# Expert outputs of a 64-image vision tower, scaled by their gate and added to the result by accumulating indirect DMAs

## The chip, the cores and the metric

The kernel runs on one core of one Trainium2 chip. The time is in device microseconds (us), the median of three runs. The engines of the core are TensorE (PE in the rows, PEld for its weight loads), VectorE (DVE), ScalarE (ACT), GpSimd (POOL) and SyncE (SP, which here only issues DMAs). Each works through its own list of instructions in order and waits for others on semaphores.

## What is computed

A small vision tower on 64 images of 3x112x112: a tokenizer (layer norm and matmul of shifted patches, 49 tokens of width 192 per image), a window attention block, and a last block with attention over the 49 tokens of an image and a mixture of eight experts. The change is in the last part of that block:

```
x = x + (o @ proj_w.T + proj_b)                      # the residual
xn2 = layernorm(x, norm2_w, norm2_b).reshape(-1, 192)
logits = xn2 @ w_gate                                # 3136 tokens, 8 experts
top_vals, top_idx = top_k(logits, 2)
gates = softmax(top_vals)
moe[t] = sum over the two chosen experts e of
         gate[t, e] * (gelu(xn2[t] @ W1[e] + b1[e]) @ W2[e] + b2[e])     # 192 -> 768 -> 192
h = h + x + moe
```

## The kernel before

Everything is in fp32. Three classes and functions write the program; class `Heads` has the last block. It begins when the window attention has left its result in memory, and goes through four stages.

**The heads stage.** 32 items, each a pair of images (128 partitions: 2 x 64, of which 49 of each 64 are real tokens), go through a software pipeline eight slots deep, written by `run_slots(eng, NP, 8, slot)` on every engine. In one slot each engine does a part of up to seven different items; the number in `item(lag)` says how many slots behind an item is. GpSimd's slot (L472 to L515) does, in this order:

- part a (newest item): six instructions of one column each, with a drain between them (L482 to L492), for the first layer norm's scale; VectorE's `bn_aggr` (L598) releases the first;
- part b (four slots behind): the multiplication with norm2's weight (L495), and, after the scatters, the addition of its bias (L507);
- part d (seven slots behind): a copy of two columns with the numbers of the destination rows into `xsrc` (L500), a drain, and two indirect DMAs (L504), which scatter the item's 128 normalized rows to the places of their first and second expert in `xs_d`, a tensor in memory sorted by expert. A row is 192 numbers and its row number (`DX = D + 1`);
- part c (three slots behind): two instructions for the second layer norm (L511, L513), for which VectorE's L591 waits, and the addition of the residual into `hall` (L515), with the semaphore `res_set`.

The gate is exp(second logit - first logit) of each token, written by ScalarE to `egs` (L758, semaphore `d_eg`). Rows that stand for no token get the row number `FAR`, which an indirect DMA skips as out of bounds.

**The turn.** VectorE counts the rows of each expert and writes a list of tiles of 128 rows (`meta`); SP and ScalarE write rows of zeros (with row number `FAR`) behind the last row of each expert (`zero_tails`); VectorE computes the two gates of each token into `gates` (L696 to L701).

**The expert stage.** 56 tiles (`NT`) of 128 rows, in a pipeline of five slots (`run_slots(eng, NT, 5, expert)`). Per tile: SP loads the rows (L963) once GpSimd has taken the row numbers of the tile two before (`xs_used`); TensorE transposes them (L913), does 12 matmuls of the first layer (L906) and 6 of the second (L921; each is shown as two, for fp32 is done in passes); ScalarE does the gelu (L801); VectorE copies the expert's first-layer weights to one of two buffers (L714, L715) and adds the output bias from PSUM into `ys` (L722, semaphore `e_out`), after the scatter of the tile two before has landed (`e_st[u]`). GpSimd (L519 to L537) waits for `e_out` and for `e_st[u]`, that of the tile two before, does an addition of one column (L527) and a copy of the row numbers (L528), drains, and scatters the tile's 128 rows to `yy_d` by an indirect DMA (L530). Then it waits for the loaded rows of a later tile and keeps their row numbers (L536, L537).

**The closing stage.** After the last scatter has landed, SP loads `yy_d` in eight groups of four items, two DMAs each (L974). ScalarE scales the second expert's rows by their gate (L814), VectorE adds the first's, scaled, and the second's to `hall` (L732, L735), and SP stores `hall` to the output (L982).

Of the kernel before, what the change touches and what calls it, by code (L numbers as in the profile page):

```python
# [16 lines left out]
F32 = mybir.dt.float32  # L17
# [31 lines left out]
NP = B // 2  # L49
# [5 lines left out]
NT = (2 * B * T + E * (ROWS - 1)) // ROWS  # L55
R = B * T + ROWS
DX = D + 1
NROW = E * R + ROWS
FAR = 1 << 20
# [18 lines left out]
C_ROW = C_TRI + P  # L78
NCONST = C_ROW + 2 * NP
# [305 lines left out]
class Heads:  # L385


    def __init__(self, nc, ctx, sb, sem, A, const, ones, colg, x2, kbd, hall, h2_d, xs_d, yy_d, out, pe1, pt1, pp, s):
        self.nc, self.A, self.const, self.ones, self.colg, self.x2, self.kbd, self.hall = nc, A, const, ones, colg, x2, kbd, hall
        self.h2_d, self.xs_d, self.yy_d, self.out = h2_d, xs_d, yy_d, out  # L390
# [5 lines left out]
        self.gates = sb("gates", [P, NP, 2])  # L396
# [35 lines left out]
        self.yl = x2[:].rearrange("p (a i k) d -> p a i k d", a=4, i=4)  # L432
        self.xdum = sb("xdum", [P, 2])
        self.yixs = sb("yixs", [P, NT], I32)
        self.yix = sb("yix", [P, 2], I32)
# [15 lines left out]
        self.o_st, self.res_set, self.d_lgo, self.xs_used, self.o_set = sem("o_st"), sem("res_set"), sem("d_lgo"), sem("xs_used"), sem("o_set")  # L451
# [3 lines left out]
        self.ew_ld, self.e_wc, self.y2_set = sem("ew_ld"), sem("e_wc"), sem("y2_set")  # L455
        self.e_st = [sem("e_st0"), sem("e_st1")]
        self.y_ld = [sem(f"y_ld{n}") for n in range(4)]
# [13 lines left out]
    def gpsimd(self, pool):  # L471
        nc, st, g = self.nc, self.st, self.nc.gpsimd  # L472
# [3 lines left out]
        def slot(item):  # L476
            a, b, c, d = item(0), item(4), item(3), item(7)
            if a:
                i = a[0]
# [16 lines left out]
            if d:  # L496
                i, u, _ = d
                pool.wait_ge(self.d_src, i + 2)
                pool.wait_ge(self.d_dst, i + 1)
                g.tensor_copy(self.xsrc[:, u, :, D:DX], self.const[:, C_ROW:C_ROW + 2 * NP].rearrange("p (i k) -> p i k", k=2)[:, bass.ds(i, 1), :].rearrange("p o k -> p k o"))  # L500
# [20 lines left out]
        def expert(item):  # L521
            if (a := item(4)):
                i, u, h = a
                pool.drain()
                pool.wait_ge(self.e_out, i + 1)
                pool.wait_ge(self.e_st[u], 16 * h)
                g.tensor_tensor(held[0], held[1], held[1], ALU.add)  # L527
                g.tensor_copy(self.yix[:, u:u + 1], self.yixs[:, bass.ds(i, 1)])  # L528
                pool.drain()
                g.indirect_dma_start(self.yy_d[:, :], bass.IndirectOffsetOnAxis(ap=self.yix[:, u:u + 1], axis=0),  # L530
                                     self.ys[:, u], None, bounds_check=2 * NP * P - 1, oob_is_err=False).then_inc(self.e_st[u], 16)
            if (b := item(1)):
                i, u, h = b
                pool.drain()  # L534
                pool.wait_ge(self.e_w[u], 16 * h + 16)
                g.tensor_tensor(held[0], held[1], held[1], ALU.add)  # L536
                g.tensor_copy(self.yixs[:, bass.ds(i, 1)], self.xs[:, u, D:DX]).then_inc(self.xs_used, 1)  # L537
        pool.wait_ge(self.dum_set, 1)
        run_slots(pool, NT, 5, expert)

    def vector(self, dve):
# [13 lines left out]
        v.memset(self.zero[:, D:DX], float(FAR))  # L555
# [139 lines left out]
        dve.wait_ge(self.d_eg, NP)  # L695
        g1, g2 = self.gates[:, :, 0], self.gates[:, :, 1]  # L696
        v.tensor_scalar(g1, self.egs[:], 1.0, None, ALU.add)
        dve.drain()
        v.reciprocal(g1, g1)
        dve.drain()  # L700
        v.tensor_tensor(g2, g1, self.egs[:], ALU.mult)  # L701
# [7 lines left out]
        def expert(item):  # L709
# [7 lines left out]
            if (c := item(3)):  # L717
                i, u, h = c
                e = dve.value_load(self.meta[0:1, 0, bass.ds(i, 1)], min_val=0, max_val=E - 1)
                dve.wait_ge(self.e_y, i + 1)  # L720
                dve.wait_ge(self.e_st[u], 16 * h)
                v.tensor_tensor(self.ys[:, u], pp[:, u, 0:D], self.b2s[:, bass.ds(e, 1), :].rearrange("p o d -> p (o d)"), ALU.add).then_inc(self.e_out, 1)  # L722
                dve.drain().then_inc(self.y_free, 1)
        run_slots(dve, NT, 5, expert)


        dve.wait_ge(self.res_set, NP)
        for n in range(NP // 4):
            dve.wait_ge(self.y_ld[n % 4], 32 * (n // 4) + 32)
            for i in range(4):  # L730
                m = 4 * n + i
                v.scalar_tensor_tensor(hall[:, m], self.yl[:, n % 4, i, 0], self.gates[:, m, 0:1], hall[:, m], ALU.mult, ALU.add)  # L732
            dve.drain()
            dve.wait_ge(self.y2_set, n + 1)
            v.tensor_tensor(hall[:, 4 * n:4 * n + 4], hall[:, 4 * n:4 * n + 4], self.yl[:, n % 4, :, 1], ALU.add).then_inc(self.o_set, 1)  # L735

    def scalar(self, act):
# [71 lines left out]

        for n in range(NP // 4):  # L810
            act.wait_ge(self.y_ld[n % 4], 32 * (n // 4) + 32)
            for i in range(4):
                y = self.yl[:, n % 4, i, 1]
                last = f(y, y, ACT.Copy, scale=self.gates[:, 4 * n + i, 1:2])  # L814
            last.then_inc(self.y2_set, 1)
# [117 lines left out]
    def sync(self, sp):  # L933
# [16 lines left out]

        sp.wait_ge(self.meta_set, 1)
# [15 lines left out]
        sp.wait_ge(self.dum_set, 1)  # L967
        for n in range(2):
            sp.wait_ge(self.e_st[n], (NT + 1 - n) // 2 * 16)

        def load(n):
            for q in range(2):
                src = self.yy_d.rearrange("(i q t k) d -> q t i k d", q=2, t=B, k=2)[q, 0:T, 4 * n:4 * n + 4]
                sp.dma_start(self.yl[q * B:q * B + T, n % 4], src).then_inc(self.y_ld[n % 4], 16)  # L974

        for n in range(4):
            load(n)
        for n in range(NP // 4):
            sp.wait_ge(self.o_set, n + 1)
            for q in range(2):  # L980
                dst = self.out.rearrange("(i q) t d -> q t i d", q=2)[q, :, 4 * n:4 * n + 4]
                sp.dma_start(dst, hall[q * B:q * B + T, 4 * n:4 * n + 4]).then_inc(self.o_st, 16)  # L982
            if n + 4 < NP // 4:
                load(n + 4)
        sp.wait_ge(self.o_st, 256)


def build(nc, A, out, stop=99):
    ctx = ExitStack()
    with ctx:  # L990
# [9 lines left out]
        def dram(name, shape, dt=F32):  # L1000
            return nc.dram_tensor(name, shape, dt, kind="Internal").ap()
# [4 lines left out]
        yy_d = dram("yy_d", [NP * P * 2, D])  # L1006
# [76 lines left out]
        heads = Heads(nc, ctx, sb, sem, A, const, ones, colg, x2, kbd, hall, h2_d, xs_d, yy_d, out, pe1, pt1, pp, s) if stop >= 4 else None  # L1083
# [435 lines left out]
def lay_out(inputs):  # L1519
# [3 lines left out]
    g = {}  # L1523
# [107 lines left out]
    c[:, C_ROW:] = (2 * (P * np.arange(NP)[None, :, None] + p[:, None, None]) + np.arange(2)).reshape(P, -1)  # L1631
# [16 lines left out]
```

## Time and profile before

| | us |
|---|---|
| median of three runs | 1308.98 |
| lowest and highest | 1304.17, 1320.23 |
| span of the profiled execution | 1321.7 |
| heads stage, first item's a part to the last one's scatter | some 608 to 980 |
| expert stage and its tail | some 990 to 1275 |
| closing stage | 1275.3 to 1321.7 |

Only the span is listed of the profiled execution, from its first to its last instruction, with nothing around it; it lies 12.7 us over the median and 1.4 us over the slowest of the three runs. TensorE's mean granted clock in it was 0.860 of full speed. Positions are us from the start of the span. In a timeline a row gives start, duration, engine, line, operation, output and inputs, and in brackets how long the engine was idle before and what released it ("issue": nothing that the profile shows, so its own drains and instruction handling). Pieces close together are merged, with their count behind the x.

### The profile page before, as it was taken

The page shows a single profiled execution, that of the slowest core. Times are in us where ns is not written, and L with a number is a line of the kernel's source. Part 1 is how long each engine was busy: PE and PEld are TensorE (multiplying, and loading weights), DVE is VectorE, ACT ScalarE, POOL GpSimd, SP SyncE. Part 2 cuts the span into 40 slices and gives each one's busy share as a digit, 9 for nine tenths or more (in the row PEclk, how much of TensorE's full clock was granted, in tenths as well). Part 3 has the DMA queues.
Part 4 walks back from the last instruction along what each step waited for, and adds up shares of the span by engine and source line. Part 5 has one row for each costly group of instructions (what it writes and reads, how often), then busy time and mean ns, then how long its engine had stood idle before and what let it go on. Part 6 is the DMA issues. An engine that isn't in the chain of part 4 may idle for free.

```text
span 1321.7 us, 25108 instructions
## 1 busy us (share of the span) xinstructions
PE 1105.6 (84%) x7254; PEld 997.7 (75%) x7255; DVE 724.3 (55%) x1825; ACT 437.7 (33%) x1092; POOL 567.1 (43%) x1075
## 2 busy tenths in 40 slices
PE   7798999899999789663999888988829999999940
PEld 4798999899998456363777777777618999999940
DVE  6566456357344888661577777787642322333224
ACT  0321221222211233421454545454304444444422
POOL 0554445444442344211355666666532444444420
PEclk9788888888888799775887889898758999999975
DMA  9545046045100200026800000000011111111114
GB/s 344 202 177 202 23 186 277 9 192 240 54 9 12 71 0 0 24 62 157 245 11 12 16 14 14 14 18 14 15 47 33 42 41 39 36 41 40 40 62 161
DMA packets 47864, 105.54 MB, mean 80 GB/s; under 512 B 6827, under 2 KB 36117, under 8 KB 45010
## 3 DMA queue, kind: packets, MB, share of 16 engines
q1 hardware_dynamic: 37986, 92.65, 20.2%
q0 software_dynamic: 5760, 9.68, 2.0%
q10 hardware_dynamic: 4080, 2.76, 0.7%
q8 instruction: 18, 0.29, 0.1%
q14 instruction: 20, 0.16, 0.0%
HBM read 87.18 MB, written 20.04 MB: 81 GB/s over the span
## 4 chain that ended last, share of the span: by engine, by line
issue 28%; PE 22%; POOLq 20%; DVE 11%; POOL 9%; DVEq 3%; DMA 3%; SPq 2%; ACT 2%; ACTq 0%
PE pe L1480 6%; POOLq L1247 5%; POOLq L534 5%; PE pe L906 4%; PE pp L921 3%; DVE prod L320 2%; POOL xs_d L504 2%; POOLq L512 2%; DVE sc L323 2%; POOLq L501 2%; DMA x<-yy_d 2%; DVEq L321 1%; POOL hall L515 1%; POOL xn L507 1%; PE pe L1484 1%
## 5 line engine op out<-in xcount | busy, mean ns | idle before, releaser
L1480 PE MATMUL pe<-wm,xm 128*128 128x193 f32 x1008 | 205.2, 372 | 1.6 <-DVEq L1333 1.6
L1480 PEld LDWEIGHTS pe<-wm,xm 128*128 128x128 f32 x1008 | 201.4, 224 | 2.7 <-issue 2.5
L906 PE MATMUL pe<-xsT,ew 96*128 96x128 f32 x1344 | 161.8, 278 | 1.5 <-ACT xsT L790 1.5
L906 PEld LDWEIGHTS pe<-xsT,ew 96*128 96x128 f32 x1344 | 159.7, 194 | 2.2 <-ACT xsT L790 2.2
L801 ACT ACTIVATE hT<-pe,eb 128x128 f32<-128x128 f32 x336 | 99.1, 366 | 154.7 <-PE pe L906 154.6
L921 PE MATMUL pp<-w2s,hT 128*128 x672 | 118.3, 326 | 0.0
L921 PEld LDWEIGHTS pp<-w2s,hT 128*128 128x128 f32 x672 | 107.8, 190 | 0.0
L530 POOL DMA_INDIRECT yy_d<-ys,yix x56 | 81.2, 1451 | 46.4 <-issue 46.4
L722 DVE TENSOR_TENSOR ys<-pp,b2s 128x192 f32<-128x192 f32 x56 | 20.0, 357 | 127.9 <-PE pp L921 127.9
L842 PEld LDWEIGHTS pp<-xT,wqk 96*96 96x96 f32 (+1 forms) x512 | 71.5, 195 | 18.7 <-issue 17.4
L504 POOL DMA_INDIRECT xs_d<-xsrc,dst x64 | 65.5, 1024 | 40.1 <-issue 40.1
L1172 ACT ACTIVATE sqt<-xm 128x2688 f32<-128x2688 f32 x14 | 34.2, 2444 | 145.2 <-DMA xm<-in_xm 42.2
L842 PE MATMUL pp<-xT,wqk 96*96 96x128 f32 (+1 forms) x512 | 79.6, 319 | 0.9 <-ACT xT L764 0.9
L1248 POOL TENSOR_TENSOR sqs<-sqs,sqt 128x448 f32<-128x448 f32 x56 | 71.2, 1271 | 8.0
L611 DVE TENSOR_TENSOR kbd<-pp,const 96x294 f32<-96x294 f32 x128 | 50.2, 451 | 27.3 <-PE pp L845 27.2
L1484 PE MATMUL pe<-ww,wv 128*128 128x193 f32 x300 | 53.4, 327 | 3.2 <-DVEq L1349 3.2
L536 POOL TENSOR_TENSOR xdum<-xdum 128x1 f32<-128x1 f32 x56 | 10.3, 184 | 101.8 <-issue 86.1
L715 DVE COPY ew<-w1s 96x1536 f32 x56 | 53.7, 958 | 0.0
L1389 DVE TENSOR_SCALAR xh<-hh,st 128x192 f32<-128x192 f32 x25 | 16.5, 662 | 67.3 <-POOL st L1269 67.3
L1484 PEld LDWEIGHTS pe<-ww,wv 128*128 128x128 f32 x300 | 49.8, 189 | 3.5 <-DVEq L1349 3.5
L714 DVE COPY eb<-b1s 128x6 f32 x56 | 9.6, 171 | 77.7 <-issue 64.7
L320 DVE TENSOR_TENSOR prod<-qkv 128x576 f32<-128x576 f32 x33 | 48.3, 1514 | 4.1 <-issue 4.1
(239 smaller groups left out, 2275.7 us busy)
## 6 DMA issues: line engine op xcount, KB each, us to landing
xm<-in_xm SPq DMA_DIRECT2D x7, 2688.0 KB, 16.6
raw<-in_xwa SPq DMA_DIRECT2D x7, 1792.0 KB, 7.2
raw<-in_xwb SPq DMA_DIRECT2D x7, 1536.0 KB, 10.4
x<-in_x SPq DMA_DIRECT2D x4, 1536.0 KB, 12.8
xs<-xs_d SPq DMA_DIRECT2D x56, 96.5 KB
x<-yy_d SPq DMA_DIRECT2D x16, 294.0 KB
w1s<-in_W SPq DMA_DIRECT2D x1, 4608.0 KB, 25.6
w2s<-in_W SPq DMA_DIRECT2D x1, 4608.0 KB, 36.5
```

Source lines behind the costliest of these rows:

```text
L320: v.tensor_tensor(prod[:, a], qkv[:, u, a:a + 1, 0:D].to_broadcast([P, 3, D]), qkv[:, u, :, D:2 * D], ALU.mult)
L504: g.indirect_dma_start(self.xs_d[:, :], bass.IndirectOffsetOnAxis(ap=self.dst[:, u, k:k + 1], axis=0), self.xsrc[:, u, k], None, bounds_ch ...
L530: g.indirect_dma_start(self.yy_d[:, :], bass.IndirectOffsetOnAxis(ap=self.yix[:, u:u + 1], axis=0), self.ys[:, u], None, bounds_check=2 * ...
L534: pool.drain()
L801: last = f(self.hT[:, u, c], pe1[:, 2 * u + c // 3, (c % 3) * ROWS:(c % 3 + 1) * ROWS], ACT.Gelu, bias=self.b1[:, u, c:c + 1])
L842: mm(pp[0:H2, g, m * P:(m + 1) * P], self.wqk[0:rows, h, g * D + m * H2:g * D + (m + 1) * H2], self.xT2[0:rows, h], start=(h == 0), stop=( ...
L906: last = mm(pe1[:, 2 * u + n // 3, (n % 3) * ROWS:(n % 3 + 1) * ROWS], self.w1[:, u, m, n * P:(n + 1) * P], self.xsT[:, m], start=(m == 0) ...
L921: last = mm(pp[:, u, 0:D], self.hT[:, u, n], self.w2s[:, bass.ds(e, 1), n * D:(n + 1) * D].rearrange("p o d -> p (o d)"), start=(n == 0), ...
L1247: pool.drain()
L1248: last = nc.gpsimd.tensor_tensor(dst, dst, src[c], ALU.add)
L1480: mm(y[:, 0:D + 1], cell(q, c), wm[:, q, c], start=(q + c == 0), stop=(q == 3 and c == KC - 1))
L1484: mm(y[:, 256:256 + D + 1], wave(wv, wv6, q), ww[:, q], start=(q == 0), stop=(q == 5))
```

## The change

Tile rows carry their gate as a 194th number. GpSimd computes it in the heads stage, the VectorE of the expert stage multiplies each output row with it, and the indirect DMA of the expert stage adds to the output tensor in memory, which SP has filled with the residual during the heads stage. `yy_d`, `gates` and the closing stage are gone. Rows for no token now have a real destination: 128 dummy rows behind the output.

In the heads stage, on GpSimd:

```diff
-DX = D + 1
+DX = D + 2
...
                 i, u, _ = d
                 pool.wait_ge(self.d_src, i + 2)
                 pool.wait_ge(self.d_dst, i + 1)
-                g.tensor_copy(self.xsrc[:, u, :, D:DX], ...)
+                pool.wait_ge(self.d_eg, i + 1)
+                g.tensor_tensor(st[:, 16:17], self.egs[:, bass.ds(i, 1)], self.ones[:, 0:1], ALU.add)
+                g.tensor_copy(self.xsrc[:, u, :, D:D + 1], ...)
             pool.drain()
             if d:
+                g.tensor_tensor(self.xsrc[:, u, 0, D + 1:DX], st[:, 16:17], self.const[:, C_NEG:C_NEG + 1], ALU.pow)
+                pool.drain()
+                g.tensor_tensor(self.xsrc[:, u, 1, D + 1:DX], self.xsrc[:, u, 0, D + 1:DX], self.egs[:, bass.ds(i, 1)], ALU.mult)
+                pool.drain()
                 for k in range(2):
                     g.indirect_dma_start(self.xs_d[:, :], ...)
```

In the expert stage, on GpSimd:

```diff
                 pool.wait_ge(self.e_out, i + 1)
-                pool.wait_ge(self.e_st[u], 16 * h)
+                pool.wait_ge(self.e_st[1 - u], 16 * (h + u))
                 g.tensor_tensor(held[0], held[1], held[1], ALU.add)
                 g.tensor_copy(self.yix[:, u:u + 1], self.yixs[:, bass.ds(i, 1)])
                 pool.drain()
-                g.indirect_dma_start(self.yy_d[:, :], ...,
-                                     self.ys[:, u], None, bounds_check=2 * NP * P - 1, oob_is_err=False)
+                g.indirect_dma_start(self.out[:, :], ...,
+                                     self.ys[:, u], None, bounds_check=B * T + P - 1, oob_is_err=True,
+                                     compute_op=ALU.add)
...
                 g.tensor_tensor(held[0], held[1], held[1], ALU.add)
-                g.tensor_copy(self.yixs[:, bass.ds(i, 1)], self.xs[:, u, D:DX]).then_inc(self.xs_used, 1)
+                g.tensor_copy(self.yixs[:, bass.ds(i, 1)], self.xs[:, u, D:D + 1])
+                g.tensor_copy(self.gxs[:, bass.ds(i, 1)], self.xs[:, u, D + 1:DX]).then_inc(self.xs_used, 1)
         pool.wait_ge(self.dum_set, 1)
+        pool.wait_ge(self.o_st, 16 * 17)
         run_slots(pool, NT, 5, expert)
```

The scatter of a tile is now issued only after that of the tile before it has landed. On VectorE:

```diff
-                v.tensor_tensor(self.ys[:, u], pp[:, u, 0:D], ..., ALU.add).then_inc(self.e_out, 1)
+                v.tensor_tensor(self.ys[:, u], pp[:, u, 0:D], ..., ALU.add)
                 dve.drain().then_inc(self.y_free, 1)
+                dve.wait_ge(self.xs_used, i + 3)
+                v.tensor_scalar(self.ys[:, u], self.ys[:, u], self.gxs[:, bass.ds(i, 1)], None, ALU.mult).then_inc(self.e_out, 1)
```

VectorE's computation of `gates` in the turn (three instructions) is removed. On SP, ahead of its wait for `meta_set`, 17 stores are added, and the loads and stores behind the last `e_st` wait are removed:

```diff
+        sp.dma_start(self.out[B * T:], self.zero[:, 0:D]).then_inc(self.o_st, 16)
+        for n in range(NP // 4):
+            sp.wait_ge(self.res_set, 4 * n + 4)
+            for q in range(2):
+                dst = self.out[0:B * T].rearrange("(i q t) d -> q t i d", q=2, t=T)[q, :, 4 * n:4 * n + 4]
+                sp.dma_start(dst, hall[q * B:q * B + T, 4 * n:4 * n + 4]).then_inc(self.o_st, 16)
         sp.wait_ge(self.meta_set, 1)
         self.zero_tails(sp, range(0, E, 2))
...
         for n in range(2):
             sp.wait_ge(self.e_st[n], (NT + 1 - n) // 2 * 16)
-        for n in range(4):
-            load(n)
-        for n in range(NP // 4):
-            sp.wait_ge(self.o_set, n + 1)
-            ...
```

The row numbers (constant `C_ROW`) now count output rows, the zero rows carry the number of a dummy row (`C_DUM`) in place of `FAR`, and the output tensor has 3136 + 128 rows, of which the first 3136 are returned.

## Rows read from the trace of the kernel before

**Rows 1.** Busy time by stage: heads, turn to the experts, experts, tail, closing stage

```profile
core 0: us, PE busy (x) PEld busy (x) DVE busy (x) ACT busy (x) POOL busy (x), PEclk, DMA share, GB/s
...
640.00:965.00 325.00, 284.07 (x2310) 238.37 (x2309) 240.07 (x873) 160.43 (x451) 193.46 (x415) 0.88 0.09 30
...
1003.50:1265.00 261.50, 261.50 (x2049) 261.50 (x2048) 77.11 (x160) 109.40 (x378) 111.32 (x266) 1.00 0.13 38
...
1275.20:1321.70 46.50, 0.00 (x0) 0.00 (x0) 18.91 (x40) 11.93 (x32) 0.00 (x0) 0.50 0.44 156
```

**Rows 2.** The closing stage in order of time: last scatter, first load, last addition

```profile
1273.05 1.00 POOL L530 DMA_INDIRECT yy_d<-ys,yix  x1 [0.82 <-issue]
1275.26 7.80 SPq L974 DMA_DIRECT2D x<-yy_d  x8
...
1315.57 0.96 DVE L735 TENSOR_TENSOR hall<-hall,x 128x768 f32<-128x768 f32 x1
```

**Rows 3.** One slot of the heads stage, GpSimd alone, in order of time

```profile
842.20 0.19 POOL L482 TENSOR_TENSOR st<-st,const 128x1 f32<-128x1 f32 x1 [0.68 <-DVE st L598]
842.53 0.55 POOL L484 TENSOR_TENSOR st<-st,const 128x1 f32<-128x1 f32 x1
843.22 0.19 POOL L486 TENSOR_TENSOR st<-st 128x1 f32<-128x1 f32 x1
843.56 0.19 POOL L488 TENSOR_TENSOR st<-st 128x1 f32<-128x1 f32 x1
...
846.35 1.08 POOL L504 DMA_INDIRECT xs_d<-xsrc,dst  x1 [0.87 <-issue]
...
850.37 0.57 POOL L513 TENSOR_TENSOR st<-st,const 128x1 f32<-128x1 f32 x1 [0.90 <-issue]
850.92 0.58 POOL L515 TENSOR_TENSOR hall<-hall,x  x1
```

**Rows 4.** First GpSimd instruction of other heads slots, with its wait

```profile
675.59 0.19 POOL L482 TENSOR_TENSOR st<-st,const 128x1 f32<-128x1 f32 x1 [3.06 <-DVE st L598]
...
686.33 0.19 POOL L482 TENSOR_TENSOR st<-st,const 128x1 f32<-128x1 f32 x1 [1.28 <-DVE st L598]
...
924.88 0.19 POOL L482 TENSOR_TENSOR st<-st,const 128x1 f32<-128x1 f32 x1 [1.84 <-DVE st L598]
```

**Rows 5.** Two items of the expert stage in order of time

```profile
1199.98 0.36 DVE L722 TENSOR_TENSOR ys<-pp,b2s 128x192 f32<-128x192 f32 x1 [2.37 <-PE pp L921]
1200.10 0.18 POOL L536 TENSOR_TENSOR xdum<-xdum 128x1 f32<-128x1 f32 x1 [1.60 <-issue]
1200.23 0.18 POOL L537 CAST yixs<-xs 128x1 f32 x1
...
1200.74 0.20 POOL L527 TENSOR_TENSOR xdum<-xdum 128x1 f32<-128x1 f32 x1 [0.34 <-DVE ys L722]
...
1201.80 0.96 DVE L715 COPY ew<-w1s 96x1536 f32 x1
1201.89 1.75 POOL L530 DMA_INDIRECT yy_d<-ys,yix  x1 [0.83 <-issue]
...
1204.26 2.81 PEld L906 LDWEIGHTS pe<-xsT,ew 96*128 96x128 f32 x24
...
1204.83 0.36 DVE L722 TENSOR_TENSOR ys<-pp,b2s 128x192 f32<-128x192 f32 x1 [2.07 <-PE pp L921]
...
1205.86 0.20 POOL L527 TENSOR_TENSOR xdum<-xdum 128x1 f32<-128x1 f32 x1 [0.28 <-issue]
...
1207.00 1.21 POOL L530 DMA_INDIRECT yy_d<-ys,yix  x1 [0.83 <-issue]
```

**Rows 6.** Tensor yy_d, all its instructions: time to landing

```profile
DMA to landing us min/median/max: 2.1/2.6/4.3
```

**Rows 7.** Chain that ended last: a load of rows from memory

```profile
990.86 1.84 DMA xs<-xs_d
```

More of the change, by code:

```diff
@@ L78 @@
 C_ROW = C_TRI + P
-NCONST = C_ROW + 2 * NP
+C_DUM = C_ROW + 2 * NP
+C_NEG = C_DUM + 1
+NCONST = C_NEG + 1
 def run_slots(eng, n, depth, slot, unroll=2):
@@ L450, in __init__ @@
         self.e_y, self.e_out, self.y_free, self.dum_set = sem("e_y"), sem("e_out"), sem("y_free"), sem("dum_set")
-        self.o_st, self.res_set, self.d_lgo, self.xs_used, self.o_set = sem("o_st"), sem("res_set"), sem("d_lgo"), sem("xs_used"), sem("o_set")
+        self.o_st, self.res_set, self.d_lgo, self.xs_used = sem("o_st"), sem("res_set"), sem("d_lgo"), sem("xs_used")
         self.h_ld = [sem(f"h_ld{n}") for n in range(4)]
@@ L454, in __init__ @@
         self.e_w = [sem("e_w0"), sem("e_w1")]
-        self.ew_ld, self.e_wc, self.y2_set = sem("ew_ld"), sem("e_wc"), sem("y2_set")
+        self.ew_ld, self.e_wc = sem("ew_ld"), sem("e_wc")
         self.e_st = [sem("e_st0"), sem("e_st1")]
-        self.y_ld = [sem(f"y_ld{n}") for n in range(4)]
     def zero_tails(self, eng, experts):
@@ L554, in vector @@
         dve.drain()
-        v.memset(self.zero[:, D:DX], float(FAR))
+        v.tensor_copy(self.zero[:, D:D + 1], const[:, C_DUM:C_DUM + 1])
         dve.drain().then_inc(self.init, 2)
@@ L693, in vector @@
         dve.drain().then_inc(self.meta_set, 1)
[L695 to L701, printed above, removed]
         for n in range(2):
@@ L721, in expert @@
                 dve.wait_ge(self.e_st[u], 16 * h)
-                v.tensor_tensor(self.ys[:, u], pp[:, u, 0:D], self.b2s[:, bass.ds(e, 1), :].rearrange("p o d -> p (o d)"), ALU.add).then_inc(self.e_out, 1)
+                v.tensor_tensor(self.ys[:, u], pp[:, u, 0:D], self.b2s[:, bass.ds(e, 1), :].rearrange("p o d -> p (o d)"), ALU.add)
                 dve.drain().then_inc(self.y_free, 1)
+                dve.wait_ge(self.xs_used, i + 3)
+                v.tensor_scalar(self.ys[:, u], self.ys[:, u], self.gxs[:, bass.ds(i, 1)], None, ALU.mult).then_inc(self.e_out, 1)
         run_slots(dve, NT, 5, expert)
-        dve.wait_ge(self.res_set, NP)
-        for n in range(NP // 4):
[L729 to L735, printed above, removed]
     def scalar(self, act):
@@ L808, in scalar @@
         run_slots(act, NT, 5, both)
[L810 to L815, printed above, removed]
     def tensor(self, pe):
@@ L1082, in build @@
         wins = Windows(nc, ctx, sb, sem, A, const, ones, xnT, wqkv, colg, mowT, owT, hall, base_d, h2_d, pe1, pt1, pp, s) if stop >= 2 else None
-        heads = Heads(nc, ctx, sb, sem, A, const, ones, colg, x2, kbd, hall, h2_d, xs_d, yy_d, out, pe1, pt1, pp, s) if stop >= 4 else None
+        heads = Heads(nc, ctx, sb, sem, A, const, ones, colg, x2, kbd, hall, h2_d, xs_d, out, pe1, pt1, pp, s) if stop >= 4 else None
         block = ctx.enter_context(nc.Block())
```

34 lines of the change are left out of this document (11 added, 23 removed).

## Prediction

> **What bounds the kernel now.** I read the busy time by stage first. Three stretches matter [rows 1]. In the heads stage (640 to 965) TensorE is busy 284 of 325 us, at a granted clock of 0.88, and no engine is full, so a chain through several engines sets the pace. In the expert stage (1003.5 to 1265) TensorE is busy 261.5 of 261.5 us at the full clock. In the closing stage (1275.2 to 1321.7) TensorE does nothing and the DMA engines are busy 0.44 of the time: it is loads, additions and stores with nothing beside them.
>
> Next the closing stage in order of time: the last scatter is issued at 1273.05, SP issues the first load when it has landed, at 1275.26, and the last addition starts at 1315.57 [rows 2].
>
> Then one slot of the heads stage on GpSimd [rows 3]. It begins at 842.20 and ends with L513 at 850.94; the part after L513 that matters goes by VectorE: L513 releases L591, VectorE comes to `bn_aggr` (L598), and that releases the next slot's first instruction. That wait, measured on GpSimd after its own last instruction, is 0.68 us in the slot shown. In the slot shown the loop is therefore nearly all GpSimd's: whatever is put between its first instruction and L513 lengthens the slot. In others the wait is longer (1.28, 1.84 [rows 4]); there VectorE was held up by TensorE, and GpSimd has that much to spare. Of the 24 slots whose first and last start at 686.33 and 924.88 [rows 4], 13 wait 0.68 us, two 0.73 and 0.75, nine 1.26 to 2.40.
>
> Last the expert stage [rows 5]. VectorE's L722 follows itself in 4.85 us, TensorE's pace. GpSimd: 1.15 us from L527 to the scatter (1200.74 to 1201.89), the scatter 1.75, then 2.22 to the next L527 (1203.64 to 1205.86); the next scatter takes 1.21, the last ones, where VectorE copies no weights, 1.00 [rows 2]. The long one starts inside the copy of the weights (1201.80, 0.96 us). Without overlap GpSimd's round would be 1.15 + 1.00 + 2.22 = 4.37 us, with full overlap 5.12, and it swings between the two to the mean of 4.85 that TensorE dictates. It has 0.48 us to spare, if it can move out of the copy's way.
>
> **Part by part.**
>
> *The closing stage goes:* 1321.7 - 1275.3 = 46.4 us [rows 2]. What stays is SP's wait for the last landing, which was there before. -46.4.
>
> *GpSimd's gate in the heads stage.* Per item: an addition of one column before the copy, a pow with drain, a multiplication with drain. The two last have their equals in the slot: pow to next 843.22 - 842.53 = 0.69, multiplication to next 843.56 - 843.22 = 0.34 [rows 3]. An undrained one-column instruction adds 0.13 (L536 to L537, 1200.10 to 1200.23 [rows 5]). That is 1.16; I take 1.25, since operands of the new ones have their column in a register, for which no row stands (bounds 1.16 and 1.35). It stands before the scatters (846.35), so both scatters, the bias addition and L513 are late by it: in the loop. In the 15 slots with no more than 0.07 to spare it costs 1.25 each, 18.6 together. In the nine with more to spare, the spare (wait minus 0.68) is 0.58 to 1.72 us, and what is left over sums to 2.3. In the tail of the stage, where fewer parts run, I count three slots at 1.25, 3.8. Together +25. Bounds: +15 if in half of the fast slots another engine has hidden slack; +36 if the spare time of the slow slots can't be used (27 x 1.35). `d_eg` of the item was set a slot earlier: that wait costs nothing. Behind the d part only GpSimd's own b and c parts queue; ScalarE waits for the scatters before it refills `xsrc`, late by the same 1.25 as all of the slot.
>
> *SP's stores of the residual.* 17 DMAs in the heads stage, where the DMA share is 0.09 [rows 1], each behind `res_set`. SP has nothing else queued until `meta_set`, and the last pair goes when item 31 has its residual, four slots before its scatter (part c against part d), with the whole turn behind that. 0, up to 2 if they delay scatters.
>
> *The turn.* The three `gates` instructions ran beside SP's zero rows: 0.
>
> *VectorE in the expert stage.* The multiplication of 128x192 is like L722 (0.36), and a drain of some 0.1 goes before it. The copy it delays ends at 1202.76 and the matmuls that read the copy start at 1204.26 [rows 5]: 1.5 us of cover for 0.5 us. 0 in the steady part; `e_out` is 0.5 late once, at the end: +0.5. The wait for `xs_used` is for a part that GpSimd did two slots before: 0.
>
> *GpSimd in the expert stage, own work.* One more copy: 0.13. The accumulating scatter has to read its destination too. The trace has no accumulating DMA. From below the scatter's 1.00 us stays as it is. From above: a plain row has a read and a write, an accumulating one two reads and a write; if the 1.00 us goes by that count it becomes 1.50. So the round without overlap is 4.50 to 5.00 us, against 4.85. I take 1.25 (round 4.75), nearer to neither: then 0.1 is to spare, some overlap with the copy is left that can't be avoided, and I take the round as 4.95: 0.1 x 54 tiles = +5. Bounds 0 and, with 5.00 and half of the overlap (0.38), 5.38: +0.53 x 54 = +28.
>
> *The new wait.* L527 now waits until the scatter before has landed. Queued behind it are the scatter, L536 and L537; SP's next load waits for L537. Issue to landing took 2.1 to 4.3 us, median 2.6 [rows 6]. Today's L527 comes 1.75 + 2.22 = 3.97 or 1.21 + 2.22 = 3.43 us after the scatter's start, so a landing up to 3.4 us is hidden. The round by this wait is landing + 1.15 + 0.1. For the landing of an accumulate, from below 2.6; from above a load (1.84 [rows 7]) in series with a scatter: 1.84 + 2.6 = 4.44, a round of 5.69, +0.84 x 54 = +45. I take 3.5, nearer the plain scatter, since a load of rows and the rows' read can overlap: round 4.75, hidden by the above, with occasional late ones (+3). At the end three scatters in a row cost 0.5 more each: +1.5.
>
> The Trainium skill, page "DMA: Bandwidth & Descriptors", section "Rules for kernel authors", says that nothing holds the bytes between an accumulate's read and its write, so the earlier DMA's semaphore must be waited for; no run here shows it, and it is why this wait can't be left out. The same page, "Latency and other measured facts", gives an HBM access 0.2 us on average and 2 us at high load; an estimate from it is a landing of 2.8 (hidden) or 4.6 (a round of 5.85, +54 us), and with a DMA share of 0.13 the first is nearer.
>
> The scatter's 1.00, 1.21 and 1.75 us by its overlap with the copy are the row. The Trainium skill, page "SBUF — State Buffer", section "Who interferes with whom", has it that a VectorE copy in a two-port mode locks GpSimd out for the whole instruction. By that rule, which the trace agrees with, GpSimd's extra work is partly taken back by moving out of the copy; were 1.75 and 1.21 the scatter's own times, the 0.13 alone would cost 0.1 x 54 = 5 us.
>
> **Sum**, against the span: -46.4 + 25 + 0 + 0.5 + 5 + 3 + 1.5 = -11.4, say -12. The span is 12.7 us over the median, mostly by TensorE's clock, which a median run shares less; the terms are the same there. 1309 - 12 = 1297.
>
> **The rivals.**
>
> 1. *The landing decides, and the kernel is slower.* Place: GpSimd's wait before L527. It begins to cost at a landing of 3.6 us (3.6 + 1.25 = 4.85) and decides the sign at 3.9 to 4.0, where 54 x 0.3 = 17 us have eaten the rest of the gain. At the 4.44 above: -46.4 + 25 + 45 + 2 = +26, 1335; if the eight rows of each DMA engine were not pipelined, far more. For: plain landings already reach 4.3 us. Against: the median is 2.6, and the DMA engines are idle. Chance 0.22.
> 2. *GpSimd's gate in the heads stage is hidden* (TensorE or VectorE sets the pace, or the clock is granted more often): -46.4 + 8 + 8 = -30, 1279. For: nine of 24 slots have the time. Against: the constant 0.68 in the others. Chance 0.2.
> 3. *GpSimd's software needs far longer for an accumulating scatter* (2.0 us for 1.00): a round of 5.5 to 5.8, +35 to +51, with the heads +25: +14 to +30, 1331. For: the 1.00 us is software time, by which rows it goes is unknown. Against: nothing in the trace. Chance 0.1.
> 4. *The change doesn't do what it says:* SP's stores come late and hold the expert stage back (GpSimd waits for all 17). Each stored group would have to be 20 us late. Chance 0.03, 1310.
>
> **How the numbers follow.** Forecast 0.45, rivals 0.22, 0.2, 0.1, 0.03. The forecast's own range is -27 (heads +15, experts +4) to +3, 1282 to 1312. The range is 1277 to 1335: below it little but rival 2 with free experts, above it the costlier half of rivals 1 and 3. A difference under 2% (26 us) is about what a measurement of this kernel can't tell from no change. Faster by over 2% needs heads and experts together under 20 us: rival 2 and the forecast's edge, 0.22. Slower by over 2%: the heavier part of rivals 1 and 3, 0.22. Within: 0.56.
>
> **What would show it.** No row after the last scatter's landing. GpSimd's L482 rows 11.1 us apart in most slots instead of 9.9, the 0.68 us wait unchanged. In the expert stage L722 4.9 to 5.0 us apart, TensorE no longer busy all the time; the accumulating scatter 1.2 to 1.5 us, landing 3 to 3.6. Wrong if the heads slots stay at 9.9 (rival 2), if L527 waits on the landing of a scatter in most rounds (rival 1), or if the scatter's own row grows to 2 us (rival 3).

## The result, and the profile after

The changed kernel takes 1360.35 us (median of four runs, 1354.43 to 1374.44) where the kernel before takes 1312.39 (four runs): the ratio is 1.0396, 95% interval 1.0346 to 1.0447. It is slower by 4%, and lies above my range of 1277 to 1335.

The span of the profiled execution is 1358.4 us, 36.7 longer than that of before. Busy time by stage of the changed kernel (heads; experts from the first scatter on; behind the last scatter), columns as in [rows 1]:

```profile
core 0: us, PE busy (x) PEld busy (x) DVE busy (x) ACT busy (x) POOL busy (x), PEclk, DMA share, GB/s
640.00:985.00 345.00, 289.81 (x2254) 244.59 (x2252) 240.55 (x865) 157.39 (x440) 217.53 (x497) 0.84 0.11 36
1030.30:1340.00 309.70, 275.80 (x2020) 260.31 (x2019) 96.28 (x211) 108.22 (x372) 134.34 (x313) 0.99 0.23 33
1354.50:1358.40 3.90, 0.00 (x0) 0.00 (x0) 0.00 (x0) 0.00 (x0) 1.57 (x1) 0.50 0.25 25
```

The closing stage is gone: 3.9 us stand behind the start of the last scatter, where before there were 48.7 (1273.05 to 1321.7 [rows 2]). But in the expert stage TensorE is no longer busy all the time, 275.8 of 309.7 us against 261.5 of 261.5 in [rows 1], at a clock of 0.99.

The heads stage went as foreseen. One slot on GpSimd, to be held against [rows 3]:

```profile
838.14 0.19 POOL L482 TENSOR_TENSOR st<-st,const 128x1 f32<-128x1 f32 x1 [0.68 <-DVE st L607]
...
841.23 0.19 POOL L501 TENSOR_TENSOR st<-egs,ones 128x1 f32<-128x1 f32 x1
...
841.69 0.55 POOL L505 TENSOR_TENSOR xsrc<-st,const 128x1 f32<-128x1 f32 x1
842.39 0.19 POOL L507 TENSOR_TENSOR xsrc<-xsrc,egs 128x1 f32<-128x1 f32 x1 [0.15 <-issue]
843.46 1.07 POOL L510 DMA_INDIRECT xs_d<-xsrc,dst  x1 [0.88 <-issue]
...
847.37 0.57 POOL L519 TENSOR_TENSOR st<-st,const 128x1 f32<-128x1 f32 x1 [0.80 <-issue]
...
849.55 0.19 POOL L482 TENSOR_TENSOR st<-st,const 128x1 f32<-128x1 f32 x1 [1.04 <-DVE st L607]
```

The wait before L482 is 0.68 us here too, and the gate's instructions (L501, L505, L507) put the first scatter 5.32 us behind L482, where it was 4.15. The 24 slots from the L482 at 667.10 to that at 939.63 take 272.5 us, against 249.3 (675.59 to 924.88 [rows 4]); most are 11.1 us, as against 9.9. The first expert scatter starts 424.7 us after the first L482 (605.62 to 1030.33), before 399.6 (607.84 to 1007.46): +25.1, and the stages ahead of it were 2.2 shorter.

The expert stage is where the forecast broke. A round on GpSimd and VectorE, in order of time, to be held against [rows 5]:

```profile
1179.89 1.58 POOL L536 DMA_INDIRECT out<-ys,yix  x1 [0.85 <-issue]
...
1183.74 0.18 POOL L543 TENSOR_TENSOR xdum<-xdum 128x1 f32<-128x1 f32 x1 [2.27 <-issue]
...
1184.00 0.17 POOL L545 COPY gxs<-xs 128x1 f32 x1
...
1184.50 0.19 POOL L533 TENSOR_TENSOR xdum<-xdum 128x1 f32<-128x1 f32 x1 [0.33 <-issue]
...
1185.65 1.60 POOL L536 DMA_INDIRECT out<-ys,yix  x1 [0.84 <-issue]
1185.93 0.36 DVE L724 TENSOR_TENSOR ys<-pp,b2s 128x192 f32<-128x192 f32 x1 [5.05 <-PE pp L908]
1186.50 0.32 DVE L727 TENSOR_SCALAR ys<-ys,gxs 128x192 f32<-128x192 f32 x1 [0.21 <-issue]
```

The scatter's own row is 1.58 us, 1.00 to 1.75 before; behind it GpSimd is idle for 2.27 us (it was 1.6) until L543. From scatter to scatter it is 5.76 us. From the first of the 56 scatters to the last it is 324.2 us (1030.33 to 1354.52), before 265.6: +58.6, or 5.89 us a tile for 4.83. The sum over the stages: -2.2 + 25.1 + 58.6 - 44.8 = +36.7.

Who waited, in the expert stage of the changed kernel (engine and line, releaser: us, times, longest):

```profile
POOL xdum L543 <- issue: 115.6, 52, 2.3
...
DVE ys L724 <- DMA out<-ys,yix: 34.5, 10, 3.6
POOL xdum L533 <- issue: 15.8, 52, 0.3
```

In ten rounds VectorE's L724 waits for a landing as well: it may write `ys` only when the scatter two tiles back has landed. L533 stands behind the new semaphore wait for the last landing, and it waits for no landing, only its usual 0.3 us. The 115.6 us stand before L543, the first instruction behind a drain, and the view calls them "issue": it shows no releaser. How long the scatters took to land, all 56:

```profile
DMA to landing us min/median/max: 3.4/3.6/4.3
```

3.6 us, where it was 2.6 [rows 6]. The landing I had forecast (3.5), and I had forecast it to be hidden.

### The profile page after: what moved, and what is told of

Its sections match the earlier page's. It is cut to its first block, busy times and chain, and to the rows that moved or that the text cites. A ratio compares the mean times of both kernels' runs of the same rounds, so it can differ in the third digit from the quotient of the medians.

```text
span 1358.4 us, 25446 instructions
## 1 busy us (share of the span) xinstructions
PE 1125.2 (83%) x7254; PEld 1004.1 (74%) x7255; DVE 731.0 (54%) x1838; ACT 426.7 (31%) x1060; POOL 623.2 (46%) x1227
## 4 chain that ended last, share of the span: by engine, by line
issue 32%; POOLq 26%; PE 14%; DVE 11%; POOL 9%; DVEq 3%; ACT 1%; SPq 1%; DMA 1%; ACTq 0%
POOLq L541 8%; PE pe L1455 6%; POOLq L1222 5%; POOLq L518 3%; DVE prod L322 2%; POOL xs_d L510 2%; DVE sc L325 2%; DVEq L323 1%; POOLq L506 1%; PE pe L1459 1%; POOL hall L521 1%; POOLq L485 1%; DVE pv L339 1%; POOL xn L513 1%; PE pp L829 1%
## 5 line engine op out<-in xcount | busy, mean ns | idle before, releaser
L1455 PE MATMUL pe<-wm,xm 128*128 128x193 f32 x1008 | 202.0, 368 | 1.6 <-DVEq L1308 1.6
L1455 PEld LDWEIGHTS pe<-wm,xm 128*128 128x128 f32 x1008 | 198.4, 221 | 2.7 <-issue 2.5
L908 PE MATMUL pp<-w2s,hT 128*128 x672 | 124.6, 336 | 28.0 <-issue 15.1
L536 POOL DMA_INDIRECT out<-ys,yix x56 | 99.3, 1773 | 47.4 <-issue 47.4
L724 DVE TENSOR_TENSOR ys<-pp,b2s 128x192 f32<-128x192 f32 x56 | 20.0, 358 | 174.4 <-PE pp L908 130.7
L543 POOL TENSOR_TENSOR xdum<-xdum 128x1 f32<-128x1 f32 x56 | 10.3, 184 | 129.3 <-issue 117.8
L843 PE MATMUL pe<-const,pm 128*128 128x128 f32 x192 | 29.2, 291 | 39.6 <-ACT pm L739 39.6
L717 DVE COPY ew<-w1s 96x1536 f32 x56 | 56.8, 1014 | 0.0
L843 PEld LDWEIGHTS pe<-const,pm 128*128 128x128 f32 x192 | 22.2, 147 | 45.9 <-ACT pm L739 45.8
L860 PE MATMUL pe<-vbd,pT 128*64 128x34 f32 x768 | 53.0, 247 | 1.6 <-ACT pT L749 1.6
```

The source lines that it names most:

```text
L536: g.indirect_dma_start(self.out[:, :], bass.IndirectOffsetOnAxis(ap=self.yix[:, u:u + 1], axis=0), self.ys[:, u], None, bounds_check=B * T ...
L717: v.tensor_copy(self.w1[:, u].rearrange("p h f -> p (h f)"), self.w1s[:, bass.ds(e, 1), :].rearrange("p o f -> p (o f)"))
L908: last = mm(pp[:, u, 0:D], self.hT[:, u, n], self.w2s[:, bass.ds(e, 1), n * D:(n + 1) * D].rearrange("p o d -> p (o d)"), start=(n == 0), ...
L1455: mm(y[:, 0:D + 1], cell(q, c), wm[:, q, c], start=(q + c == 0), stop=(q == 3 and c == KC - 1))
```

## The experiments

The kernel before ran beside each group of these, with medians of 1308 to 1320 us; where a ratio is given, it is to those runs. Times without a ratio are one run. The heads stage of the same code differs between profiles (391.7 to 399.0 us in e4, e5 and e7, 424.7 to 427.6 in the changed kernel, e1, e6 and e8), so I read each profile by stages as well: "heads" is from the first L482 (or the line it has there) to the first expert scatter, "experts" from that to the last scatter's start, "rest" what follows. Each stage time is from one profile.

| kernel | time | heads | experts | rest |
|---|---|---|---|---|
| before | 1312.4 | 399.6 | 265.6 | 48.7 |
| changed | 1360.4 | 424.7 | 324.2 | 3.9 |
| e1 plain scatter | 1297.0 | 427.5 | 265.7 | 2.8 |
| e2 two targets, no wait | 1360.1 | 429.3 | 327.1 | 3.9 |
| e3 gate in the kernel before | 1346.5 | 428.0 | 265.4 | 48.0 |
| e4 gate elsewhere | 1317.9 | 399.0 | 313.0 | 3.9 |
| e5 e4 and index work elsewhere | 1276.6 | 393.0 | 267.8 | 3.9 |
| e6 no drain behind the scatter | 1313.1 | 425.8 | 282.9 | 3.9 |
| e7 e5 with a plain scatter | 1260.1 | 391.7 | 265.2 | 2.7 |
| e8 half the rows | 1332.2 | 427.6 | 302.0 | 3.5 |
| e9 no wait, no drain | 1304.4 | 431.8 | 264.4 | 6.5 |
| e10 kernel before, one drain less | 1311.9 | 394.1 | 265.8 | 48.0 |
| e11 e5 and e10 | 1273.2 | 398.1 | 266.8 | 4.0 |
| e12 wait, no drain | 1325.6 | 440.4 | 268.5 | 6.4 |

First theory: the accumulating scatter costs GpSimd itself more time, in its instruction and in the drain behind it. Rivals: the new wait for the landing, the added copy, the bounds flag.

**e1, the scatter without accumulation.**

```diff
-                                     ..., oob_is_err=True, compute_op=ALU.add)
+                                     ..., oob_is_err=True)
```

> The changed kernel with the accumulation taken out of the expert scatter (the rows are written over the residual, so the sum is left out); wait, gate, copies and the bounds flag stay. Theory (an accumulating scatter costs GpSimd itself some 1.2 us more: 0.59 in the instruction, 0.6 in the drain behind it): instruction back to 1.0 to 1.75 us, landing 2.6, round 4.85 to 4.95 in place of 5.78, time some 1360 - 55 * 0.85 = 1313. Rival (the round is made by the wait for the landing, the added copy or the bounds flag): round stays above 5.5 us, time over 1345.

1296.95 us, experts 265.7. With everything of the change in place but the accumulation, the expert stage takes what it took before. (That the whole time is also my forecast for the change, 1297, is chance: the forecast had 9.5 us for the expert stage, which are not there.) The copy, the flag and the wait cost nothing beside a plain scatter; 58 us hang on the accumulation. GpSimd's rows of two rounds:

```profile
1181.86 1.52 POOL L536 DMA_INDIRECT out<-ys,yix  x1 [0.85 <-issue]
...
1185.01 0.29 POOL L542 TENSOR_TENSOR xdum<-xdum 128x1 f32<-128x1 f32 x1 [1.63 <-issue]
...
1187.00 1.02 POOL L536 DMA_INDIRECT out<-ys,yix  x1 [0.85 <-issue]
...
1189.64 0.18 POOL L542 TENSOR_TENSOR xdum<-xdum 128x1 f32<-128x1 f32 x1 [1.62 <-issue]
```

Scatter to L542 is 3.15 and 2.64 us, against 3.85 in the changed kernel.

**e2, two targets, the wait of before.**

```diff
-                pool.wait_ge(self.e_st[1 - u], 16 * (h + u))
+                pool.wait_ge(self.e_st[u], 16 * h)
-                g.indirect_dma_start(self.out[:, :], ...
+                g.indirect_dma_start((self.alt if u else self.out)[:, :], ...
```

> The changed kernel with odd tiles accumulated into a second tensor, also filled with the residual (so half of the addition is left out of the output), and with the wait of before (the scatter two tiles back) in place of the wait for the last one. Theory (GpSimd's own time per accumulating scatter is the round; the wait is hidden): round 5.7 to 5.8 us, time 1355 to 1362, GpSimd free of waits on landings. Rival (the wait for the landing makes the round): round back to 4.9 to 5.1, time some 1315.

SP fills both targets with the residual, which doubles its stores in the heads stage (in e9 and e12 too). 1360.12 us, experts 327.1: taking away the semaphore wait alone gains nothing. That speaks for the theory, but, as e6 shows, only because something else waits for the same thing.

**e3, the gate alone.** The three instructions (addition, pow, multiplication, two drains) put into the kernel before, results in a spare column.

> The kernel before with the three GpSimd instructions of the gate (addition, pow with drain, multiplication with drain) added at their place in the heads stage, their results unused. Theory (the heads stage's loop goes through GpSimd, 1.19 us a slot): slots 11.1 us in place of 9.9, +20 to +23 us on the kernel before. Rival (the heads stage of the changed kernel was longer by TensorE's clock or by SP's stores): under +8 us.

Ratio to the kernel before 1.023 (interval 1.015 to 1.031), some 30 us, with heads 428.0. The loop goes through GpSimd; the price was above my 20 to 23. Over all profiles the eight kernels with the gate on GpSimd have heads of 424.7 to 440.4 us (mean 429), the six without 391.7 to 399.6 (mean 396): 33 us, or 31 without e2, e9 and e12, where SP stores the residual twice. The granted clock, over the same 24 slots of before, of the changed kernel and of e7 (gate elsewhere), a fence each, in this order:

```profile
675.60:924.90 249.30, 222.23 (x1835) 188.17 (x1835) 189.68 (x697) 128.26 (x360) 156.24 (x337) 0.90 0.04 15
```

```profile
667.10:939.60 272.50, 233.25 (x1828) 197.54 (x1827) 194.21 (x697) 129.04 (x360) 177.88 (x408) 0.86 0.06 20
```

```profile
660.80:906.50 245.70, 217.20 (x1832) 183.32 (x1830) 190.52 (x697) 130.84 (x384) 156.35 (x336) 0.92 0.07 22
```

With longer slots TensorE is busy for a smaller part of them, and it has the lower of its two clocks, 1.2 GHz, more often (0.86 of 2.4 GHz on average against 0.90 and 0.92). Over the same slots of the other kernels it is 0.80 to 0.84 with the gate on GpSimd and 0.89 to 0.94 without. That the longer slots cause the lower clock is not shown by a run of its own.

**e8, half of the rows.** The scatter takes partitions 0 to 63 only.

> The changed kernel with the accumulating scatter over 64 of the 128 rows of a tile (half of the expert outputs is left out). If GpSimd's cost goes by the row, the instruction falls from 1.59 to about 0.8 to 1.0 us and the drain behind it from 2.2 to 1.4 to 1.7, the round to 4.85 to 5.0, time some 1315. If it is a fixed cost of each accumulating DMA, both stay and the round stays at 5.7.

In between: the instruction 1.43 us for 1.58 where no copy lengthens it, landing 3.2 for 3.6, experts 302.0. Half of the rows takes off 22 of the 58.6 us, so most of the cost is per scatter, not per row. What GpSimd's queue carried (packets, MB, share of the 16 engines' span), page of before, of the changed kernel, of e8:

```profile
q0 software_dynamic: 5760, 9.68, 2.0%
```

```profile
q0 software_dynamic: 11136, 10.39, 5.0%
```

```profile
q0 software_dynamic: 7552, 7.63, 3.5%
```

Before, 120 scatters had 48 packets each; with 64 x 48 of the heads stage taken off, an accumulating one has 144, and with half the rows 80.

**e4, the gate off GpSimd.** ScalarE writes exp(d) and exp(-d) of the logit difference d as the 194th number, VectorE makes 1/(1+w) of it per tile.

```diff
-                f(self.egs[:, bass.ds(n6, 1)], self.st[:, 12:13], ACT.Exp).then_inc(self.d_eg, 1)
+                f(x[:, 0, D + 1:DX], self.st[:, 12:13], ACT.Exp)
+                f(x[:, 1, D + 1:DX], self.st[:, 12:13], ACT.Exp, scale=-1.0).then_inc(self.d_eg, 1)
...
+                v.tensor_scalar(self.gx[:, u:u + 1], self.gxs[:, bass.ds(i, 1)], 1.0, None, ALU.add)
+                dve.drain()
+                v.reciprocal(self.gx[:, u:u + 1], self.gx[:, u:u + 1])
```

> The changed kernel with the gate off GpSimd's list in the heads stage: ScalarE writes exp(d) and exp(-d) of the logit difference d into the row (one more instruction of 0.2 us), VectorE makes 1/(1+w) of it for each tile in the expert stage (two one-column instructions). Theory (GpSimd is the loop of the heads stage): slots back to 9.9 us where TensorE's clock is full, time 22 to 30 us under the changed kernel, some 1333. Rival (ScalarE or VectorE take over the loop): under 10 us gained. The expert round stays at 5.8 in both.

1317.93 us, heads 399.0, ratio to the kernel before 1.0024 (0.9973 to 1.0075): the heads stage is back, 42 us below the changed kernel. The profiles differ by 45 us: 26 in heads, 8 ahead of it, where the code is the same, and 11 in the expert stage, which I had not expected. The 56 scatters' own rows are shorter there, 1606 ns on average against 1773, which is 56 x 0.167 = 9 us (by line, e4 and the changed kernel; ahead of the bar busy time, mean ns):

```profile
L532 POOL DMA_INDIRECT out<-ys,yix x56 | 89.9, 1606 | 47.3 <-issue 47.3
```

```profile
L536 POOL DMA_INDIRECT out<-ys,yix x56 | 99.3, 1773 | 47.4 <-issue 47.4
```

In both kernels 50 of the 56 scatters overlap VectorE's copy of the weights (0.96 us); what differs is which of the two starts first. In e4 the copy starts 0.01 to 0.53 us after the scatter in 47 of them, and both take their usual time (1.58 to 1.61 and 0.95 to 0.98 us). In the changed kernel both keep their usual time in 26 (the copy starts 0.01 us before to 0.54 after the scatter); in 11 the copy starts first, and the scatter takes 1.95 to 2.30 us; in ten it starts 0.54 to 0.73 us after the scatter, which then takes 1.92 to 1.94, and the copy 1.13 to 1.30. Why the order is another one in e4 no run shows.

**e5, GpSimd's list emptied.** VectorE picks out row numbers and gates (`e_w` wait, two one-column instructions beside the weights' copy, one more beside the bias), GpSimd keeps:

```diff
                 pool.wait_ge(self.e_out, i + 1)
                 pool.wait_ge(self.e_st[1 - u], 16 * (h + u))
                 g.tensor_tensor(held[0], held[1], held[1], ALU.add)
                 pool.drain()
                 g.indirect_dma_start(self.out[:, :], ..., compute_op=ALU.add).then_inc(self.e_st[u], 16)
```

> The kernel of e4 with the row numbers and gates of a tile picked out by VectorE, so that GpSimd's list in the expert stage is one dummy addition that holds the waits, a drain and the accumulating scatter. Theory (GpSimd's own list is the round: 0.75 for the three copies, 1.15 to the scatter, 1.59, 2.2): the list falls to about 4.6, but the wait for the landing (3.65 after the scatter's start) and 1.0 to the next one give 4.75 to 5.0; time 1276 to 1290, below the kernel before. Rival (something else holds the round at 5.8): no change against e4.

1276.58 us, ratio to the kernel before 0.9695 (0.9610 to 0.9781), nothing left out: faster than both. Now the waits name the DMA:

```profile
POOL xdum L528 <- DMA out<-ys,yix: 108.8, 54, 2.2
...
DVE ys L715 <- PE pp L902: 43.6, 54, 2.9
```

GpSimd waits 108.8 us for landings here too, but it has nothing else to do: landing (3.6) and its 1.15 us fit into TensorE's 4.85, and VectorE waits for TensorE, as before.

**e6, the drain behind the scatter removed** (the one at the head of the part with L543 to L545; the drain ahead of the next scatter's waits stays).

> The changed kernel without GpSimd's drain right behind the scatter; the drain before the next scatter's waits stays. If the 2.2 us behind the instruction are GpSimd's own work on the descriptors, they only move to the next instruction or the next drain and the round stays at 5.7 to 5.8. If they are the drain's (waiting for something that the three copies needn't), the copies move up beside it and the round falls by 0.3 to 0.7, time 1320 to 1345.

1313.05 us, experts 282.9: 41 us for one drain, far more than expected. The rows:

```profile
1178.61 1.59 POOL L537 DMA_INDIRECT out<-ys,yix  x1 [0.84 <-issue]
...
1180.00 0.43 POOL L545 TENSOR_TENSOR xdumb<-xdum 128x1 f32<-128x1 f32 x1
...
1180.26 0.40 POOL L547 COPY gxs<-xs 128x1 f32 x1
...
1182.39 0.19 POOL L534 TENSOR_TENSOR xdum<-xdum 128x1 f32<-128x1 f32 x1 [1.73 <-DMA out<-ys,yix]
...
1183.54 1.94 POOL L537 DMA_INDIRECT out<-ys,yix  x1 [0.84 <-issue]
```

The three one-column instructions (L545 to L547) start 1.39 us after the scatter does, and they run: GpSimd is not busy with the scatter. Then L534 waits, named, for the landing, 3.78 us after the scatter. So the theory falls: the time behind the instruction isn't GpSimd's work. I then took the landing of single scatters and set it beside the next instruction behind the drain. One of the changed kernel (the scatter at 1179.89, L543 at +3.85) and one of e1 (the scatter at 1187.00, L542 at +2.64):

```profile
DMA to landing us min/median/max: 3.6/3.6/3.6
```

```profile
DMA to landing us min/median/max: 2.4/2.4/2.4
```

In 17 scatters of the changed kernel, 13 of e1, 11 of e8 and 21 of the kernel before, landings from 2.4 to 4.3 us, the next instruction came 0.2 to 0.3 us after the landing, in every one. The traces say the same of all the others: in the changed kernel, the kernel before, e2, e3, e4, e8 and e10 it is 0.18 to 0.27 us in all 55 scatters of the expert stage that another instruction follows, with landings from 2.1 to 5.5 us; in e1 in 54 of 55 (0.91 in one of the last, where the next instruction is L533, which waits for VectorE too). The drain's own row does not show the wait. In the chain that ended last, behind the scatter of 1179.89 in the changed kernel, it ends with the scatter's row, and 2.12 us follow for which the view names no work:

```profile
1179.66 1.81 POOLq L541
1181.47 2.12 issue
1183.59 0.04 POOLq L542
```

L541 is the drain, L542 the semaphore wait behind it. The new theory: a GpSimd drain behind an indirect DMA waits until that DMA has landed.

**e7, e5 with a plain scatter.**

> The kernel of e5 with a plain scatter in place of the accumulating one (the addition is left out). It shows what is left when neither the heads stage nor the scatter costs anything: TensorE's round of 4.85, 46 us less closing stage, time some 1265. If the heads stage has not come back, some 1290.

1260.08 us, heads 391.7, experts 265.2: the floor. e5 loses 2.6 us to it in the expert stage.

**e9 and e12, no drain in the expert loop.** GpSimd orders the copy before the scatter by a semaphore of its own; e9 has two targets and the old wait, e12 one target and the new wait.

```diff
-                pool.drain()
...
-                g.tensor_copy(self.yix[:, u:u + 1], ...)
-                pool.drain()
+                g.tensor_copy(self.yix[:, u:u + 1], ...).then_inc(self.c_s, 1)
+                pool.wait_ge(self.c_s, i + 1)
+                g.tensor_tensor(self.xdumc[:, 0:1], held[1], held[1], ALU.add)
```

> The changed kernel with no drain on GpSimd in the expert loop (a semaphore that GpSimd gives and takes itself orders the row numbers' copy before the scatter), two targets as in e2 (half of the addition is left out of the output) and the wait for the scatter two tiles back. In every kernel so far the drain behind a scatter ended 0.22 to 0.30 us after that scatter's landing. Theory (the landing is waited for twice, by the drain and by the new semaphore wait, and only both together hold GpSimd back; without both GpSimd has some 1.6 + 1.5 us of work a round): TensorE's round of 4.85, time 1295 to 1302, as e1. Rival (the accumulate costs GpSimd the time itself): round over 5.3, time over 1325.

> As e9, but with one target and the changed kernel's wait for the last scatter's landing: nothing is left out. Theory: landing 3.6 + 0.25 to the next held instruction + 0.6 to 1.0 to the next scatter = 4.5 to 5.0 us a round; time 1298 to 1312. Rival as in e9.

e9: 1304.43 us, experts 264.4, TensorE busy throughout, with accumulating scatters of 1.6 to 2.2 us:

```profile
1032.00:1290.00 258.00, 258.00 (x2021) 258.00 (x2020) 92.52 (x210) 108.29 (x374) 161.93 (x372) 1.00 0.28 40
```

The accumulation costs nothing once nobody on GpSimd waits for its landing. e12: experts 268.5 (4.88 us a tile), so with the semaphore wait alone the landing nearly fits into TensorE's round. Its time of 1325.6 was outside what I expected, by its heads stage (440.4). There its code is that of e9 (431.8) and e2 (429.3); all three store the residual twice, although e12 uses only one target, and all three are above the 424.7 to 427.6 of the kernels that store it once. So part of it may be those stores; the rest is the spread of that stage between profiles. No run separates the two.

**e10, one drain of the heads stage in the kernel before**, the one between L511 and L513, replaced by a semaphore in the same way.

> The kernel before with one drain replaced, the one between the two one-column instructions of part c in the heads stage, by a semaphore that GpSimd gives and takes itself. It is the first drain behind the two scatters. Theory (it waits for the second scatter's landing, 2.64 us after its start): L513 0.5 to 0.7 us earlier, slots 9.3 in place of 9.9 where GpSimd is the loop, 8 to 18 us faster. Rival (GpSimd itself is busy with descriptors, or the drain costs what a semaphore costs): within 4 us of the kernel before.

The rows of e10, and below them the second scatter of the slot in [rows 3]:

```profile
846.68 0.97 POOL L505 DMA_INDIRECT xs_d<-xsrc,dst  x1 [0.30 <-issue]
...
848.22 0.20 POOL L512 TENSOR_TENSOR st<-st,const 128x1 f32<-128x1 f32 x1
848.50 0.57 POOL L514 TENSOR_TENSOR st<-st,const 128x1 f32<-128x1 f32 x1
...
850.60 0.19 POOL L483 TENSOR_TENSOR st<-st,const 128x1 f32<-128x1 f32 x1 [0.97 <-DVE st L599]
```

```profile
847.73 0.97 POOL L504 DMA_INDIRECT xs_d<-xsrc,dst  x1 [0.30 <-issue]
```

L514 (L513 of before) starts 1.82 us after the second scatter, 0.6 us before that scatter landed (2.4 us after its issue), where L513 started 2.64 us after it before (847.73 to 850.37 [rows 3]). So this drain waited for the landing too. The time: ratio 0.9971 (0.9926 to 1.0017), no difference that was measured: with 0.8 us gone from GpSimd's part, the next wait for VectorE is 0.97 us and the slot 9.7.

**e11, e5 with e10's edit.**

> The kernel of e5 with the drain of e10 replaced. Theory: 8 to 18 us under e5, so 1260 to 1268, some 4 per cent under the kernel before. Rival as in e10: as e5, 1276.

1273.22 us, ratio to the kernel before 0.9692 (0.9623 to 0.9761): as e5, within what can be told.

## Why the prediction was wrong, point by point

*The closing stage:* forecast -46.4, measured -44.8. Right.

*GpSimd's gate:* forecast +25 (bounds 15 and 36), in the pair of profiles +25.1, over all kernels +33. The mechanism was right (11.1 us slots, 0.68 us waits unchanged, e3, e4). The pair's agreement is partly luck: I let the slots with spare time absorb the 1.25 us, and did not count with a lower clock. Of the eight kernels with the gate on GpSimd the changed one has the shortest heads stage and the highest granted clock over those 24 slots (0.86, the others 0.80 to 0.84).

*SP's stores, the turn, VectorE's multiplication, the added copy:* forecast 0 or less than 1; e1 has all of them and an expert stage of 265.7 against 265.6, and e3, which has no stores, has a heads stage of 428.0 against 424.7 to 427.6. Right. e1's time of 1297 equals the forecast by chance: with its 9.5 us for the expert stage taken out, the forecast would be some 1288.

*The accumulating scatter on GpSimd:* forecast 1.25 us, bounds 1.00 and 1.50; measured 1.58, outside. But e9 shows that this alone costs nothing.

*The landing:* this is the step that failed. I wrote that today's L527 comes 3.97 or 3.43 us after the scatter's start, "so a landing up to 3.4 us is hidden". The landing was 3.6, close to my 3.5. But L527 came that late because of the landing: the drain before L536 had waited for it, and 1.6 us after each scatter were put down in my sum as GpSimd's fixed round of 4.37. With the landing in series, the round is 3.6 + 0.25 to L543, 0.76 to L533, 1.15 to the scatter: 5.76, as measured. My landing of 3.5 put in that place would have given 5.66, and 54 x (5.66 - 4.85) = +44 us where the sum had 5 + 3 for the whole of GpSimd's part. The view had called this wait "issue", and I took "nothing that the profile shows" for the engine's own time.

*Rival 1* had the price (a slower kernel by the landing in series, 5.69 us a round for 4.44) and the wrong place: it was to happen at the semaphore wait before L527. e2 takes that wait away and gains nothing, e6 takes the drain away and gains 41 us, e9 takes both and has the whole excess back. With the drains gone and the semaphore wait left (e12) the landing costs 2.9 us (268.5 for 265.6), so of that wait by itself I was nearly right. *Rival 3* (GpSimd's software) had the instruction's own row at 2.0 us; it is 1.58, and e9 carries it at no cost. *Rival 2* fell with e3. *Rival 4* did not come: SP issued the last of its stores at 981 us, and the first GpSimd instruction behind the wait for them (L543 at 1013.15) was released by the load of the first tile's rows.

The estimate that I had worked out from a figure of the Trainium skill (page "DMA: Bandwidth & Descriptors", section "Latency and other measured facts", 0.2 us for an HBM access on average) was a landing of 2.8 us; the runs show 3.6, and the measurement decides. The Trainium skill's rule on the shared port (page "SBUF — State Buffer", section "Who interferes with whom") has it that whichever of the two issues first gets the port pair for its whole instruction and blocks the other. For a scatter that starts inside VectorE's copy the trace agrees: 1.95 to 2.30 us in place of 1.58. For a copy that starts with the scatter or up to 0.5 us after it, the trace does not agree: neither takes longer (26 times in the changed kernel, 47 in e4).

## What to carry to other kernels

Idle time that a profile calls "issue" is not thereby the engine's own: before it goes into a sum as a constant, set it beside the landing of the DMA issued just before, over several instances; if the two move together, it is a wait, and it grows with the DMA. In a loop like this one, with an indirect DMA on GpSimd, keep drains out of the stretch between the DMA and its landing (a semaphore that the engine gives to itself orders two of its instructions without that wait), and give index work to another engine. And a stage whose pace is a loop through one engine's small instructions pays for each instruction added, once per slot.

## What the runs showed of the hardware that I had not expected

- Behind a GpSimd drain that follows an indirect DMA, the next instruction started 0.2 to 0.3 us after that DMA's landing, plain (2.1 to 4.5 us) or accumulating (3.0 to 5.5 us), whatever the landing was. Without the drain the next GpSimd instruction starts 1.39 us after a 1.59 us scatter does. That it is the drain that waits is concluded from this and from e6, e9 and e10; its own row in the profile ends with the scatter's.
- Clear of VectorE's copy, an accumulating scatter of 128 rows of 768 bytes lands 3.5 us after its start and a plain one to the same tensor 2.4 (e1; to `yy_d` in the kernel before 2.15). It takes 1.58 instead of 1.02 us to issue, and makes 144 packets for 48; with 64 rows it still takes 1.43 and 3.1 us.
- A scatter that starts inside VectorE's copy of the weights takes longer (in the changed kernel 1.95 to 2.30 us for 1.58); one that starts with the copy or up to 0.5 us ahead of it does not, and neither does the copy.
